# Feed-forward first layer of a decoder block: the small-part products on 64 rows, two feature groups side by side

## The reference, cut to what matters

```python
# x: (16, 256, 256), U1 (256, 64), V1 (64, 1024), U2 (1024, 64), V2 (64, 256)
P = jnp.einsum('bsd,dr->bsr', x, U1)
H = jax.nn.gelu(jnp.einsum('bsr,rf->bsf', P, V1) + b1)
Q = jnp.einsum('bsf,fr->bsr', H, U2)
return jnp.einsum('bsr,rd->bsd', Q, V2) + b2
```

## Time and profile before

| what | us |
|---|---|
| median of 3 runs | 586.6 (586.26 to 589.58) |
| profiled execution, its own time | 589.89 |
| its span, first to last instruction | 588.1 |
| PE busy | 536.4 |
| DVE busy | 405.6 |
| ACT busy | 344.7 |
| POOL busy | 278.7 |

### The profile page before, as it was taken

How to read it: one execution, slowest core, us unless ns; L and a number is a source line. 1 busy time by engine, 2 the same in 40 slices (tenths; PEclk the granted TensorE clock), 3 DMA queues, 4 the chain that set the end, 5 groups by cost and what they waited for, 6 DMA issues and landing times.

```text
span 588.1 us, 11834 instructions
## 1 busy us (share of the span) xinstructions
PE 536.4 (91%) x4236; PEld 367.9 (63%) x4236; DVE 405.6 (69%) x912; ACT 344.7 (59%) x505; POOL 278.7 (47%) x317
## 2 busy tenths in 40 slices
PE   6996989999999999999999999999797678999993
PEld 3884767676767676767767676767464345555551
DVE  6578786969687878788787869696967521344444
ACT  3452556566666666666757575666565566565651
POOL 6566344464655554637374655545441122242424
PEclk9998899999999999999999999999997889999997
DMA  8653111204020302021113202120101010032322
GB/s 268 142 111 74 37 31 57 69 1 103 4 85 7 98 9 78 29 77 30 57 33 73 77 10 57 49 69 1 32 4 31 18 55 19 26 119 93 121 89 107
DMA packets 29130, 35.99 MB, mean 61 GB/s; under 512 B 5720, under 2 KB 15320, under 8 KB 29080
## 3 DMA queue, kind: packets, MB, share of 16 engines
q1 hardware_dynamic: 28216, 34.37, 20.2%
q10 hardware_dynamic: 864, 0.95, 0.5%
HBM read 23.51 MB, written 8.65 MB: 55 GB/s over the span
## 4 chain that ended last, share of the span: by engine, by line
PE 60%; DVE 16%; issue 13%; POOL 5%; ACT 4%; DMA 1%; POOLq 1%; SPq 0%; ACTq 0%
PE FR L1158 20%; PE BK L1158 8%; PE BK L1326 8%; DVE nmax L989 7%; PE SC L1283 5%; PE SC L1311 4%; PE FR L1243 3%; PE FR L1371 2%; PE FR L1221 2%; DVE lin_tm L900 2%; POOL rs L604 2%; POOL c_fm L609 2%; PE BK L1343 2%; PE SC L1158 2%; DVE y L1025 2%
## 5 line engine op out<-in xcount | busy, mean ns | idle before, releaser
L989 DVE TENSOR_REDUCE nmax<-SC 128x4 f32<-128x1024 f32 x128 | 156.1, 1220 | 31.8 <-PE SC L1283 30.9
L718 ACT ACTIVATE probs<-SC 128x1024 f32<-128x1024 f32 x128 | 130.9, 1023 | 70.1 <-PE SC L1311 69.9
L1326 PE MATMUL BK<-probs,v_aug 128*32 128x256 f32 x1024 | 70.5, 393 | 0.6 <-ACT probs L718 0.6
L1283 PE MATMUL SC<-k_blk,q_grp 48*128 48x512 f16 x256 | 51.4, 399 | 18.3 <-DVE nmax L989 18.3
L522 POOL TENSOR_TENSOR rs<-ve,minus_half 128x2 f32<-128x2 f32 x16 | 11.2, 700 | 95.3 <-DVE nm L1031 95.3
L499 POOL TENSOR_TENSOR att_fm_l<-att_raw,att_fm_h 128x512 fp32r<-128x512 f32 x16 | 20.5, 1283 | 74.6 <-ACT att_raw L693 74.6
L1311 PE MATMUL SC<-q_grp,k_blk 64*128 64x256 f16 x512 | 50.5, 275 | 3.4 <-ACT q_grp L675 1.8
L811 ACT ACTIVATE probs<-SC,b_ff 128x512 f32<-128x512 f32 x64 | 39.8, 686 | 22.5 <-PE SC L1532 21.7
L1326 PEld LDWEIGHTS BK<-probs,v_aug 128*32 128x32 f32 x1024 | 27.0, 111 | 26.4 <-issue 14.9
L1283 PEld LDWEIGHTS SC<-k_blk,q_grp 48*128 48x128 f16 x256 | 12.4, 93 | 46.0 <-DVE nmax L989 24.6
L1311 PEld LDWEIGHTS SC<-q_grp,k_blk 64*128 64x128 f16 x512 | 25.0, 97 | 21.5 <-ACT probs L718 4.3
(11 more groups left out here) (234 smaller groups left out, 1560.0 us busy)
## 6 DMA issues: line engine op xcount, KB each, us to landing
x_fm<-in_x_fm SPq DMA_DIRECT2D x16, 256.0 KB, 5.7
x_tm<-in_x_tm SPq DMA_DIRECT2D x16, 256.0 KB, 5.3
x_kept<-x2b SPq DMA_DIRECT2D x16, 256.0 KB, 2.3
x_tm<-x_kept SPq DMA_DIRECT2D x16, 256.0 KB, 2.7
out<-c_fm SPq DMA_DIRECT2D x16, 256.0 KB, 2.0
c_fm<-in_c_fm SPq DMA_DIRECT2D x15, 256.0 KB, 6.4
k_blk<-k_rope SPq DMA_DIRECT2D x128, 16.0 KB, 1.8
cos_t<-rope_tables SPq DMA_DIRECT2D x8, 128.0 KB
```

The source lines that it names most:

```text
L718: act.activation(probs[:, j % 4], SB[:], ACT.Exp, scale=SCALE).then_inc(s_exp, 1)
L989: dve.tensor_reduce(nmax[:, t, :, 2 * q:2 * q + 2], src[:].rearrange("p (s f) t -> p s f t", s=2), AX.X, ALU.max, negate=True).then_inc(s_ ...
L1283: mm = pe.matmul(out[:, 2 * s:2 * s + 2].rearrange("p h t -> p (h t)"), q_grp[n % NB][rows, q, t * P:(t + 1) * P], k_blk[n % NB][rows, q]. ...
L1326: mm = pe.matmul(BK[q // 2][HP * k:HP * (k + 1), (q % 2) * T:(q % 2 + 1) * T], v_aug[b % NB][:, t, HC * q + k], probs[:, j % 4, k], start= ...
```

## The change

The second product of each group, V1lo × P, is now taken over 64 rows: V1lo × Phi alone. Two feature groups form a pair. The first group's product uses rows 0 to 63 of `w_v1[1]` and of `p_fm`; the second group's uses rows 64 to 127 of `w_v1[1]` and a copy of the block's 64 x 512 hi part in the upper rows, `p_up`, which lies over `cs_fm`. So a pair is now: two products over 128 rows with the hi weights, then two products over 64 rows in the two halves of the array. `h_ff` is called once for a pair, waits for gelu f-3 ahead of everything, and at f = 0 waits for the copy `s_p_up` between the two kinds. DVE makes the copies: that of block 0 after the attention pipeline's last step and before `stats2(14)`, that of block 1 after `ev_p(15)` and before `ffn_block(0)`, that of block i+1 at the head of loop pass i, when block i's first-layer products are done.

```diff
+        p_up = flat2(cs_fm[0][:])
...
+            dve.wait_ge(s_v2_mm, B)
+            dve.wait_ge(s_k2_mm, B)
+            dve.wait_ge(s_p_ev, 2)
+            dve.tensor_copy(p_up[R:P], p_fm[0:R, 0:FB]).then_inc(s_p_up, 1)
             stats2(LAST - 1)
             att_norm(LAST)
             add2(LAST)
             ev_p(LAST - 1)
             stats2(LAST)
             ev_p(LAST)
+
+            def raise_p(i):
+
+                wait_apart(dve, s_h_mm, NF * i)
+                dve.wait_ge(s_p_ev, 2 * i + 2)
+                dve.tensor_copy(p_up[R:P], p_fm[0:R, bass.ds(i * FB, FB)]).then_inc(s_p_up, 1)
...
+            raise_p(1)
             ffn_block(0)
-            with dve.Fori(1, NFB) as i:
+            with dve.Fori(1, NFB - 1) as i:
+                raise_p(i + 1)
                 ffn_block(i)
+            ffn_block(NFB - 1)
...
             def h_ff(i, f):
-                wait_apart(pe, s_gelu, NF * i + f + 1)
-                out = SC[f % 4 // 2][:].rearrange("p h t -> p (h t)")[:, FB * (f % 2):FB * (f % 2) + FB]
+                wait_apart(pe, s_gelu, NF * i + f + 2)
+                out = [SC[f % 4 // 2][:].rearrange("p h t -> p (h t)")[:, FB * k:FB * (k + 1)] for k in range(2)]
+                tok = bass.ds(i * FB, FB)
                 for k in range(2):
-                    mm = pe.matmul(out, w_v1[k][:, f * P:(f + 1) * P], p_fm[:, bass.ds(i * FB, FB)],
-                                   start=(k == 0), stop=(k == 1))
-                mm.then_inc(s_h_mm, 1)
+                    pe.matmul(out[k], w_v1[0][:, (f + k) * P:(f + k + 1) * P], p_fm[:, tok], start=True, stop=False)
+                if f == 0:
+                    wait_apart(pe, s_p_up, i + 1)
+                for k, p in enumerate((p_fm[0:R, tok], p_up[R:P])):
+                    pe.matmul(out[k], w_v1[1][R * k:R * k + R, (f + k) * P:(f + k + 1) * P], p,
+                              start=False, stop=True).then_inc(s_h_mm, 1)
...
                 for f in range(0, NF, 2):
                     h_ff(i, f)
-                    h_ff(i, f + 1)
```

More of the change, by code:

```diff
@@ L70, in wait, with flat2 @@
         eng.wait_ge(sem, value)
+def flat2(ap):
+    return ap.rearrange("p a b -> p (a b)")
 def build(nc, a):
@@ L226, in build @@
         s_att_hi, s_att_raw = sem("s_att_hi"), sem("s_att_raw")
+        s_p_up = sem("s_p_up")
         s_x1_hi, s_p_hi, s_qf_hi = sem("s_x1_hi"), sem("s_p_hi"), sem("s_qf_hi")
@@ L1569, in _ @@
             h_ff(0, 0)
-            h_ff(0, 1)
             att_t(LAST)
             h_ff(0, 2)
-            h_ff(0, 3)
             u2_ff(0, 0)
             h_ff(0, 4)
-            h_ff(0, 5)
             x2_t(LAST - 1)
@@ L1581, in _ @@
             h_ff(0, 6)
-            h_ff(0, 7)
             u2_ff(0, 4)
```

## The result

The changed kernel takes 597.1 us (median of 6, 592.49 to 599.78) against 586.99 (median of 6) before: ratio 1.0155, 95% interval 1.0108 to 1.0203, so +9.1 us by the ratio. The forecast was 595.1.

The account below looks back on a forecast made before the run. Bound: how soon a pair's first group reaches ACT (A and C), not PE's work. Block 1 +2.4 and blocks 2 to 7 +6.1 give +8.5 us on 586.6: 595.1, range 590.0 to 599.0.

Parts of the forecast that it names:

- A: Block section from start of h0 to h4, paced by gelus: 0.43 us longer, from 3.15 to 3.58.
- B: Block section from start of h4 to h6, with no gelu in its way: 0.16 us longer, before 3.58.
- C: Block section from start of h6 to the next h0, paced by gelus: 0.43 us longer, from 3.15 to 3.57.
- Pitch: Start of h0 to the next block's h0 in the loop: 10.9 us instead of 9.88.
- Gelu 0 of block 1: First gelu of block 1, held by DVE's copy queued behind ev_p(15): 1.81 us later, at 509.59 instead of 507.78.
- The price of a change of shape: TensorE switching between 128-row and 64-row products: 0.09 us gap plus 0.11 for weights not loaded ahead, together 0.20.
- The side-by-side price: A pair's two 64-row products run at once in 0.23 us, saving one product per pair, 0.93 per block on PE.
- the rival without overlap: The pair's 64-row products do not run at once for this dtype: +11 us, 597.6; chance 14%.
- The rival with free packing: PE is the bound and packing costs nothing: 32 pairs save 7.5 us, 579.1; chance 4%.
- The halfway rival: Each change of shape costs 0.10 us: +5.7, 592.3; chance 18% together with the case of free changes.
- The free wait for gelu f-3: The pair's stricter wait ahead of h costs nothing, since earlier waits on PE already cover it.
- the cost without cover: DVE's copy in blocks 2 to 7, if not hidden: up to 0.45 us per block; it was forecast as covered.

Follow-up runs that it names:

- order_only: Kernel before with only the pair's order (two hi products, then two lo), all on 128 rows, no copy: ratio 1.0064, stretch 100.35 us against 97.05.
- shape_only: Kernel before, its order kept, each lo product on 64 rows alone, nothing side by side: ratio 1.0316, stretch 114.84 us against 97.05.
- pack_mid: Changed kernel with v2's halves behind h3 and h7, later copies between v2's halves on DVE, block 1's ahead of ev_p(15): ratio 1.0018 to before.
- copies_only: Kernel before plus only DVE's copies and the wait for them, h unchanged: ratio 1.0049, stretch 100.28 us against 97.05.
- v2_late: Changed kernel, block 1's copy ahead of ev_p(15), v2 moved behind h7, later copies behind Q's lo part: ratio 1.0076 to before.
- uniform_rows: Kernel with all of h on 64 rows in side-by-side steps, three DVE copies a block: ratio 1.0337 to before.
- copy_early: Changed kernel with block 1's copy moved ahead of ev_p(15) on DVE: ratio 1.0134 to before, stretch 104.28 us against the changed kernel's 105.51.
- uniform_rows_v2_halves: All of h on 64 rows with three DVE copies, v2's halves behind h3 and h7, DVE alternating adds and statistics: ratio 1.0311 to before.

## Why the prediction was right

Step by step, forecast and then measured. The pair's load 0.66 after h0: 0.67. Gelu 0 1.25 after h0: 1.27. A 3.58: 3.59. B 3.74: 3.73. C 3.57: 3.58. Pitch 10.90: 10.90. Block 1 begins later by 0.59: 0.53 (15.71 from the first h product instead of 15.18). Of this the delay through ACT's table load is 0.44, as said, and the pair h4 of block 0 added 0.10, not 0.16 (from its first product to wo(15) 1.50 instead of 1.40). Gelu 0 of block 1 later by 1.81: the wait that I placed there is in the trace, 1.41 us against "about 1.4", and the gelu comes 18.51 after the first h product instead of 16.73, +1.78. Block 1's whole +2.40: 12.43 instead of 10.58 and the 0.53, +2.38. ACT's idle time ahead of the gelus, up: 30.7 instead of 22.5. Sum +8.5: +8.46.

The mechanism was that A and C are chains through ACT. order_only shows it by itself. The price of a change of shape, 0.20, was read from an attention part in another shape mix; shape_only and pack_mid show it in place. The side-by-side price, which only f16 rows had shown, held: the rival without overlap (597.6) falls by the starts at 514.00. The rival with free packing falls twice, by order_only and by pack_mid. The halfway rival (0.10 a change) falls by shape_only. The free wait for gelu f-3 is borne out by order_only, which has it: its PE waits for nothing between h0 and h3.

One term was mis-sized, and did no harm: I had the copy done by 536.3, 0.5 after the statistics' end. At the head of a loop pass it starts 0.6 after them and takes up to 0.71. I had put the cost without cover at up to 0.45 a block; copies_only measured 0.39. That the copy stayed covered all the same was in part luck: the cover was the changed kernel's own loss in C and the pair's later need of the copy.

One reading was careless. I wrote that PE is at 8 or 9 tenths in the last ten slices and ACT at 5 or 6; the slices of PE are 7 6 7 8 9 9 9 9 9 3, and ACT's last is 1. Only the loop is at 9. No term of the sum rests on it.

The runs' median is 2.0 above the forecast. The stretch accounts for 8.46 of the 9.1 by the ratio, whose interval (6.3 to 11.9 us) covers the rest.

## What to carry to other kernels

Before cutting work on the busiest engine, ask which instruction's end the next engine waits for: a reorder that leaves the work alone cost 3.3 us here, and v2's halves moved into two waits gained 2.1 (0.25 of it by DVE's new order, behind the last v2). Packing two half-height products saved one product's time in full where the stream of h kept one shape (B 1.90 instead of 2.13); each change of shape (0.20) eats most of a 512-column product (0.23). When attributing a small change in a long kernel, compare from an instruction where the two programs part, not the spans.

## What the runs showed of the hardware that I had not expected

A 64x512 copy on DVE took 0.42 us in most places, inside the loop too (every one of v2_late, pack_mid and uniform_rows). At the head of a loop pass in the changed kernel, in copy_early and in copies_only it took 0.67 to 0.71 from block 3 on, and there it and POOL's line 610 lengthened together. DVE and POOL of copies_only:

```profile
523.10 0.67 DVE L1146 CAST cs_fm_h<-p_fm 64x512 fp32r x1 [0.60 <-issue]
523.46 0.86 POOL L610 TENSOR_TENSOR rs<-ve,minus_half 128x2 f32<-128x2 f32 x1
```

Line 610 takes 0.68 to 0.70 wherever no copy is beside it. All copies of 0.67 and more have it beside them; beside line 615 alone a copy took 0.42 to 0.53, and beside line 528 it took 0.42 while line 528 took 0.93 instead of 0.70. So what POOL does at that moment goes with the length of a copy, and a copy with the length of POOL's instruction. What in the two instructions decides it is open. Open too is why the copy at the head of a pass begins 0.56 to 0.60 after the instruction ahead of it, in time that the profile books as issue.

Weights for both halves of the rows load at once (two loads at 514.00), and within one shape on 64 rows they are ahead of the products: steps stay 0.23 apart.

Waits of about 2.4 us for DVE in uniform_rows were followed by stretches at the lower clock level (1.2 GHz; steps 0.43 apart), which made one late subtraction cost more than its own wait. Not every such wait was: in uniform_rows_v2_halves the granted clock fell after a wait of 2.16 us (0.87 over block 2) and not after the next one, of 2.88 (1.00 over block 3).
